# Six local-attention layers of a 2048-token kernel: the value path is folded into per-head weights and applied to the shifted input, and half of the softmax exponentials are taken straight from PSUM

## What is computed

```python
qkv = x @ Wqkv                     # 128 -> 3 * 1024; 16 heads of 64
q = l2norm(q) * qs ; k = l2norm(k) * ksc
q, k = rotary(q), rotary(k)
# windows of 32 queries, each with the 64 keys of its own and the window before
sim  = einsum(bq, bk2) * 8 ; sim = where(mask, -max, sim)
attn = softmax(sim)
out  = (attn @ bv2) @ Wo           # 1024 -> 128, added to x
x    = x + a * gelu(gate) @ W2 + b2     # after a layer norm and W1
```

## Time and profile before

| | |
|---|---|
| three runs | 2907.69, 2910.03 and 2917.73 us; median 2910.03 |
| span of the profiled execution | 2911.7 us |
| PE busy | 2789.5 us (96%) |
| DVE busy | 2336.3 us (80%) |
| ACT busy | 1746.4 us (60%) |
| POOL busy | 1680.3 us (58%) |

### The profile page before, as it was taken

How to read it: one execution, slowest core, us unless ns; L and a number is a source line. 1 busy time by engine, 2 the same in 40 slices (tenths; PEclk the granted TensorE clock), 3 DMA queues, 4 the chain that set the end, 5 groups by cost and what they waited for, 6 DMA issues and landing times.

```text
span 2911.7 us, 98296 instructions
## 1 busy us (share of the span) xinstructions
PE 2789.5 (96%) x40886; PEld 1832.5 (63%) x40886; DVE 2336.3 (80%) x3830; ACT 1746.4 (60%) x2618; POOL 1680.3 (58%) x1454
## 2 busy tenths in 40 slices
PE   8999999999999999899999999999999999999997
PEld 5556565655665655566656666666666666666665
DVE  6777755774677776998968999889998999898884
ACT  4455555555666665556666666666666666666663
POOL 1000002000466665676767888878887888788882
PEclk9999999999999999999999999999999999999999
DMA  3000000000011111243234434333443343333332
GB/s 97 1 1 1 1 1 3 1 1 10 21 45 46 45 46 31 77 129 79 73 103 106 99 86 114 84 93 88 114 95 91 92 118 91 88 89 83 89 85 66
DMA packets 183114, 188.24 MB, mean 65 GB/s; under 512 B 77517, under 2 KB 130515, under 8 KB 181139
## 3 DMA queue, kind: packets, MB, share of 16 engines
q1 hardware_dynamic: 182675, 181.94, 24.8%
HBM read 61.00 MB, written 6.03 MB: 23 GB/s over the span
## 4 chain that ended last, share of the span: by engine, by line
PE 73%; DVE 10%; issue 5%; POOL 5%; SPq 3%; ACT 3%; DMA 1%; DVEq 0%; POOLq 0%; ACTq 0%
PE ps L1348 13%; PE ps L587 13%; PE ps L1356 5%; PE ps L1400 5%; PE ps L1442 4%; PE ps L1363 4%; PE ps L622 4%; PE ps L600 4%; PE ps L1389 2%; PE ps L1456 2%; PE ps L1409 2%; PE ps L534 2%; PE ps L605 2%; PE ps L1457 2%; DVE nmx L695 2%
## 5 line engine op out<-in xcount | busy, mean ns | idle before, releaser
L1348 PE MATMUL ps<-wqkv,xcT 128*128 128x512 f32 x1152 | 553.2, 603 | 4.7 <-DVE area L1886 1.6
L587 PE MATMUL ps<-xnT,qp 128*128 128x512 f32 (+3 forms) x1280 | 527.1, 543 | 17.2 <-ACT prob L814 16.3
L2030 POOL TENSOR_TENSOR ra<-ra,rb 128x1024 f32<-128x1024 f32 x191 | 452.4, 2375 | 121.9 <-DVE rb L1854 121.0
L814 ACT ACTIVATE prob<-ps,ebias,shift 128x1024 f32<-128x1024 f32 (+7 forms) x384 | 360.3, 955 | 124.0 <-DVE ebias L704 60.4
L822 ACT ACTIVATE probT<-ps 128x512 f32<-128x512 f32 (+3 forms) x384 | 207.9, 541 | 353.6 <-PE ps L600 353.5
L587 PEld LDWEIGHTS ps<-xnT,qp 128*128 128x128 f32 x1280 | 231.7, 191 | 273.6 <-issue 228.5
L2049 POOL TENSOR_TENSOR ra<-ra,rn 128x1024 f32<-128x1024 f32 x192 | 362.3, 1908 | 8.9 <-DVE ra L1946 1.2
L695 DVE TENSOR_REDUCE nmx<-ps 128x1 f32<-128x1024 f32 (+7 forms) x256 | 245.8, 987 | 108.3 <-PE ps L587 93.3
L1348 PEld LDWEIGHTS ps<-wqkv,xcT 128*128 128x128 f32 x1152 | 196.7, 190 | 154.3 <-issue 143.5
L1630 ACT ACTIVATE sq<-ps 128x1024 f32<-128x1024 f32 x192 | 195.6, 1019 | 85.6 <-PE ps L1348 85.3
L1852 DVE TENSOR_TENSOR ra<-ps,tab 128x1024 f32<-128x1024 f32 x192 | 233.6, 1217 | 3.7 <-issue 3.1
(11 more groups left out here) (274 smaller groups left out, 5651.9 us busy)
## 6 DMA issues: line engine op xcount, KB each, us to landing
vw<-vs SPq DMA_DIRECT2D x576, 130.0 KB
vw<-vs SPq DMA_DIRECT2D x384, 65.0 KB
bc<-bc_scratch SPq DMA_DIRECT2D x128, 128.0 KB, 2.9
area<-bc_scratch SPq DMA_DIRECT2D x128, 128.0 KB, 4.3
wqkv<-lwqkv_dram SPq DMA_DIRECT2D x6, 1536.0 KB, 8.6
xc<-xs SPq DMA_DIRECT2D x96, 32.0 KB
wo<-lwo_dram SPq DMA_DIRECT2D x6, 512.0 KB, 9.6
xc<-xs SPq DMA_DIRECT2D x96, 31.8 KB
```

The costliest lines, as they stand in the source:

```text
L587: mm = E.matmul(ps[:, 2 * r + o // 512, 0:w], k.qp[:, group % 2, g % NTH * P:(g % NTH + 1) * P], k.xnT[:, k0 + o:k0 + o + w], start=True, ...
L814: A.activation(k.prob[:, r, 0:nk], ps[:, 2 * r:2 * r + 2, :].rearrange("p a b -> p (a b)")[:, 0:nk], ACT.Exp, bias=k.ebias[:, row % 2:row ...
L1348: mm = E.matmul(to[:, c, :], k.xcT[:, n % 4, :], k.wqkv[l % 2][:, at + 512 * c:at + 512 * (c + 1)], start=True, stop=True)
L2030: G.tensor_tensor(k.ra[:, n % 2, w, :], k.ra[:, n % 2, w, :], k.rb[:, w, :], ALU.add).then_inc(s("added_" + what), 1)
```

## The change

Values are no longer projected. Per layer and head the product of `Wv` and `Wo` (128x128) is formed once (`fold`); per tile the probabilities, normalised and transposed by DVE in blocks of 32x32, weigh the shifted input itself (`mix`: eight matmuls of 32 rows, 128 columns and 512 moving columns), and the 16 heads' results go through the 16 folded matrices in `side`. The first eight heads take their exponential from PSUM with the negated maximum as bias, one ACT instruction of 64 columns per head; for the other eight DVE subtracts as before. The rotary product is one DVE instruction of 2048 columns, POOL's sum two of 512. The sums of squares are one reduction. The bias b2 becomes a row of ones in the forward block's product (`FROWS`) and its POOL additions go. The copy of the recurrence's state goes from DVE to ACT (`state`). The orders of all queues and the PSUM pairs change with it, and the recurrence starts one step later (`FIRST_UNIT` 22 to 23).

```diff
@@ tables @@
-TAPS = {3: 3, 4: 3, 5: 3, 6: 2, 7: 3, 8: 3, 9: 2, 10: 2, 11: 3, 12: 3, 13: 2, 14: 1}
+TAPS = {4: 3, 5: 3, 6: 3, 7: 3, 8: 3, 9: 3, 10: 2, 11: 3, 12: 3, 13: 2, 14: 2}
-        a, b, c, d = (3, 1, 2, 0) if n % 2 else (0, 1, 2, 3)
...
+        a, b, c, d = (2, 3, 0, 1) if n % 2 else (0, 1, 2, 3)
+        table.update({("scores", n): a, ("q", n + 2): b, ("late", n): d, ("k", n + 2): c, ("extra", n): d, ("side", n): a, ("rows_q", n + 1): b, ("rows_k", n + 1): c,
+                      ("mix0", n): a, ("mix1", n): b})
+FOLDS = {0: (("late", 0, 0), ("extra", 0, 1))}
+FOLDS.update({NT * (l - 1) + 8 + half: (("late", l, half),) for l in range(1, L) for half in range(2)})
@@ PE @@
+    def scores(n):
+        to = pair(("scores", n), ("shifted_s", n + 1), ("exp_s", n + 1))
...
+    def fold(place, n, l, half):
...
+                mm = E.matmul(to[:, o, j * P:(j + 1) * P], k.wvT[at, 4 * half + j, :], k.wo[at, 4 * half + j, :], start=True, stop=True, skip_group_check=True)
+    def mix(n):
+        to = [pair((f"mix{i}", n), ("mixT", 2 * n + i + 1)) for i in range(2)]
+        E.wait_ge(s("prT"), n + 1)
...
+        for half in range(2):
+            for w in range(4):
+                at = slice(WIN * w, WIN * (w + 1))
+                of = k.xc[at, n % XRING, :] if half == 0 else k.xp[at, n % PRING, :]
+                mm = E.matmul(to[w // 2][:, w % 2, :], of, prT[at, :, 1 - half, :], start=half == 0, stop=half == 1, skip_group_check=True)
@@ PE, side @@
-            for c in range(8):
-                mm = E.matmul(to[:, 0, 0:P], k.oT[:, c * P:(c + 1) * P], k.wo[:, l % 2, c, :], ...)
+            for c in range(H):
+                mm = E.matmul(to[:, 0, 0:P], k.mixT[:, c, :, :].rearrange("p w q -> p (w q)"), k.wvo[:, l % 2, c, :], ...)
@@ PE, a step: scores, q, late, k, extra/forward, side, rows, mix @@
-            turn_probs(n)
-            project("v", n + 1, ("v_out", n + 2))
-            values(n, 0)
-            values(n, 1)
-            turn_out(n)
+            scores(n)
+            project_q(n + 2)
...
+            project_k(n + 2)
...
+        forward(n)
...
+            side(n)
...
+            mix(n)
@@ ACT, a step @@
+            mix_out(n - 1, 0)
+            mix_out(n - 1, 1)
             square("q", n + 2)
+                state(u)
             unit_decay(k, u)
...
             probs(n)
             square("k", n + 2)
-            values_out(n + 1)
...
-            out_turned(n)
             lengths(n + 2)
@@ ACT, probs @@
+        of = pair("scores", n)[:, 0, :]
+        A.wait_ge(s("top_s"), n + 1)
...
+        for j in range(8):
+            ins = A.activation(k.pr[:, j * DH:(j + 1) * DH], of[:, j * DH:(j + 1) * DH], ACT.Exp, bias=k.nmxl[:, n % 2, j:j + 1])
+        ins.then_inc(s("exp_s"), 1)
+        A.wait_ge(s("shifted_s"), n + 1)
+        A.activation(k.pr[:, 512:1024], k.pr[:, 512:1024], ACT.Exp).then_inc(s("exp"), 1)
@@ DVE @@
+    def normalise(n):
+        pr = k.pr[:].rearrange("p (h d) -> p h d", d=DH)
+        V.wait_ge(s("exp"), n + 1)
+        V.tensor_reduce(k.suml[:], pr, X_AXIS, ALU.add).then_inc(s("v"), k.v.up())
+        V.reciprocal(k.recl[:], k.suml[:]).then_inc(s("v"), k.v.up())
+        V.tensor_tensor(pr, pr, bcast(k.recl[:], 2, DH), ALU.mult).then_inc(s("v"), k.v.up())
...
+        V.transpose(k.prT[:], k.pr[:]).then_inc(s("prT"), 1)
@@ DVE, rotate @@
-        V.tensor_tensor(out_a, of, bcast(tab[:, 2 * w, :], 1, H), ALU.mult)
-        V.tensor_tensor(out_b[:, :, 0:32], ...)
-        V.tensor_tensor(out_b[:, :, 32:64], ...).then_inc(s("rotated_" + what), 1)
+        V.tensor_tensor(k.rot[:, n % 2, w, :, :].rearrange("p c (h d) -> p c h d", d=DH), bcast(heads(what, n), 1, 2),
+                        bcast(k.tab[:, n % FRAME, 2 * w:2 * w + 2, :], 2, H), ALU.mult).then_inc(s("rotated_" + what), 1)
@@ DVE, a step @@
+            scan(u)
             shift(n)
+            rotate("q", n + 2)
+            rotate("k", n + 2)
+            normalise(n)
             finish(n - 1)
...
+            gated(m, int(what[2]))
...
+            sum_squares(n + 2)
@@ POOL, add @@
-        G.tensor_tensor(k.ra[:, n % 2, w, :], k.ra[:, n % 2, w, :], k.rb[:, w, :], ALU.add).then_inc(s("added_" + what), 1)
+        G.tensor_tensor(a[:, :, 0:DH // 2], a[:, :, 0:DH // 2], b[:, :, DH // 2:DH], ALU.add)
+        G.tensor_tensor(a[:, :, DH // 2:DH], a[:, :, DH // 2:DH], b[:, :, 0:DH // 2], ALU.add).then_inc(s("added_" + what), 1)
@@ SP @@
-    def spread_values(n):
+    def keys_before(n):
+        S.wait_ge(s(f"xc{n % 2}"), 48 * (n // 2 + 1))
...
+            S.dma_start(k.xp[0:WIN, b, :], k.xc[P - WIN:P, (n - 1) % XRING, :]).then_inc(s(f"xp{n % PRING}"), 16)
+        S.dma_start(k.xp[WIN:P, b, :], k.xc[0:P - WIN, n % XRING, :]).then_inc(s(f"xp{n % PRING}"), 16)
```

More of the change, by code:

```diff
@@ L44 @@
 SCANS = 9060
-VALUE_HEADS = [2 * (2 * c + i) + o for i in range(2) for o in range(2) for c in range(4)]
-OUT_HEADS = [2 * (2 * c + i) + o for o in range(2) for i in range(2) for c in range(4)]
+XRING, PRING = 8, 4
 class Count:
@@ L1405, in turn_out @@
-    def turn_out(n):
-        to = pair(("turn_out", n), ("oT", n + 1))
-        E.wait_ge(s("on1"), n + 1)
-        for c in range(8):
-            mm = E.transpose(to[:, c // 4, c % 4 * P:(c % 4 + 1) * P], k.on[:, c * P:(c + 1) * P], k.ident[:])
-        mm.then_inc(s("out_turned"), 1)
+        for j in range(8):
+            for w in range(4):
+                for o in range(2):
+                    mm = E.matmul(to[WIN * w:WIN * (w + 1), o, j * DH:(j + 1) * DH], k.qT[o * DH:(o + 1) * DH, j, WIN * w:WIN * (w + 1)],
+                                  k.kT[o * DH:(o + 1) * DH, n % 2, j, WIN * w:WIN * w + DH], start=False, stop=True, skip_group_check=True)
@@ L1530, in project_in @@
     def project_in(place, n, m):
-        to = pair((place, n), ("in_out", 2 * m + 2))
+        to = pair((place, n), ("in_out", 2 * IN_ORDER.index(m) + 2))
         for q in range(2):
@@ L1669, in probs, with mix_out, state @@
     def probs(n):
-        for o in range(2):
-            here = k.pr[:, o * 512:(o + 1) * 512]
-            A.wait_ge(s("shifted_s"), 2 * n + o + 1)
-            A.activation(here, here, ACT.Exp).then_inc(s("exp"), 1)
-    def out_turned(n):
-        A.wait_ge(s("out_turned"), n + 1)
+        of = pair("scores", n)[:, 0, :]
+        A.wait_ge(s("top_s"), n + 1)
+        if n:
+            A.wait_ge(s("prT"), n)
+        for j in range(8):
+            ins = A.activation(k.pr[:, j * DH:(j + 1) * DH], of[:, j * DH:(j + 1) * DH], ACT.Exp, bias=k.nmxl[:, n % 2, j:j + 1])
+        ins.then_inc(s("exp_s"), 1)
+        A.wait_ge(s("shifted_s"), n + 1)
+        A.activation(k.pr[:, 512:1024], k.pr[:, 512:1024], ACT.Exp).then_inc(s("exp"), 1)
+    def mix_out(n, i):
+        A.wait_ge(s("mixed"), 2 * n + i + 1)
         if n:
             A.wait_ge(s("fin_mm"), n)
-        A.activation(k.oT[:], flat("turn_out", n), ACT.Copy).then_inc(s("oT"), 1)
+        A.activation(k.mixT[:, :, 2 * i:2 * i + 2, :].rearrange("p c w q -> p w c q"), pair(f"mix{i}", n).rearrange("p w (c q) -> p w c q", q=WIN), ACT.Copy).then_inc(s("mixT"), 1)
+    def state(u):
+        c, i, b = u // NS, u % NS, u % 2
+        A.wait_ge(s("scanned"), u + 1)
+        A.activation(k.last[:, i, :], k.hx[:, b, :, CH - 1], ACT.Copy).then_inc(s("state"), 1)
     def normal_turned(m):
@@ L1763, in transformer_act @@
             unit_decay(k, u)
-        if n + 3 < NTILE:
-            turned_input(n + 3)
-        if new_frame(n + 1) and n + 1 < NTILE:
-            halo_turned(n + 1)
+        if n in IN_LATE:
+            projected_in("late", n, IN_LATE[n])
+        if n == FACTOR_STEP:
+            factors(n)
+        if n in RATE_STEPS:
+            rates(n, RATE_STEPS[n])
+        for place, l, half in FOLDS.get(n, ()):
+            folded(place, n, l, half)
         if n < NTILE:
@@ L1994, in transformer_dve @@
             down(m - 1)
-        elif what and what != "turn_normal" and not gate_first:
-            gated(m, int(what[2]))
         if n == NTILE + 3:
@@ L2324 @@
     qs, ks = a["L1_ffn_q_scale"], a["L1_ffn_k_scale"]
-    turned = lambda v: np.concatenate([v[:, DH // 2:], v[:, :DH // 2]], 1)
-    by_heads = lambda v, axis, order: np.concatenate([np.take(v, range(DH * h, DH * h + DH), axis) for h in order], axis)
     b1 = np.zeros((L, P, 6), np.float32)
```

361 lines of the change are left out of this document (139 added, 222 removed).

## The result

The changed kernel takes 3150.34 us (four runs, 3146.01 to 3158.49) against 2912.2 us for the kernel before beside it: a ratio of 1.083 [1.080, 1.086], 238 us slower. The forecast was 3035 with a range to 3110. The direction was right, and the loss is nearly twice the one predicted.

The account below looks back on a forecast made before the run. PE bounds the kernel before; after the change a loop through PE, ACT and DVE would: 64 steps at 19.1 and 31 at 18.1 us, plus convolution and folds, 1813 against 1686, less 1.5 at the tail: 3035 us, range 2785 to 3110.

Parts of the forecast that it names:

- The loop closes: Links through PE, ACT and DVE run one after another each step: 19.1 us with a unit, 18.1 without; chance 0.49.
- the first rival: PE's or DVE's work, not the chain of waits, sets the step; with DVE at 16.5 us, 2795 us; chance 0.28.
- Both idle times: PE idle some 3 us ahead of each `mix`, DVE some 2 us ahead of the keys' rotary product.
- The gain of PE's shorter work: PE's work per step falls by 5.4 - 1.9 - 2.0 = 1.5 us.
- Line 1: Residual (`finish`), which frees the PSUM pair that `mix` takes, and its semaphore: 0.3 us.
- Line 2: `mix` on PE, eight 32-row matmuls of 512 columns: 2.0 us, ends 1.7 and 6.9.
- the fourth rival: `mix` row groups do not overlap, or idle PE gets its lower clock: over 3400 us; chance 0.05.
- Lines 3 and 4: On PE, mask and scores 2.1 us, then query projection to the end of its last result 1.98 us.
- line 7: Eight ACT exponentials of 64 columns: 2.0 us, at 0.25 us each, ends 0.21 and 0.30.
- Line 6: The recurrence's decays and state copy on ACT: 0.95 us together, only in steps that have a unit.
- Line 12: DVE's product of the probabilities, both inputs in SBUF, waits for POOL's sum: 1.05 us, ends 0 and 1.2.

Follow-up runs that it names:

- the edit of PE's order: Changed kernel with `side(n)` put ahead of `forward(n)` on PE in steps with n % 4 == 2, from step 6 on: 3101.87 us.
- the useless matmuls: Changed kernel with twelve extra bfloat16 matmuls of 512 columns on PE ahead of `mix`, results unused, in three steps of four: 3091.63 us.
- the experiment with the reduction: Changed kernel with DVE's product that divides the probabilities replaced by a sum of the same 1024 columns: 3029.1 us.
- the version of 2897 us: Changed kernel with keys' square ahead of the exponentials, one exponential of 1024 columns, and `side` early in steps with n % 4 == 2: 2897.15 us.

## Why the prediction was right, and where it failed

**The loop closes** (the forecast against the first rival): right in its mechanism. Both idle times that were to show it are there, and moving the keys' square alone brings 160 us. The gain of PE's shorter work was never collected.

The links, as mean distances over 92 steps of the trace (start to start; line 1 from the end of DVE's transpose to `mix`), beside the prediction's lines:

| lines of the prediction | predicted us | measured us |
|---|---|---|
| 1, from the transpose over the residual to `mix` | 0.3 | 0.98 |
| 2, `mix` | 2.0 | 2.59 |
| 3, mask and scores | 2.1 | 2.05 |
| 4, query projection, with its semaphore | 1.98 | 2.18 |
| 5 and 6, queries' square, decays, state | 1.85 | 1.77 |
| 7 and 8, the exponentials | 2.5 | 2.09 |
| 9, keys' square | 1.0 | 1.08 |
| 10, rotary product of the keys | 2.2 | 2.21 |
| 11, sum and reciprocal | 1.4 | 1.53 |
| 11 and 12, product with its wait | 2.25 | 2.34 |
| 11, transpose | 1.2 | 1.25 |
| 13, the semaphore not in a link | 0.3 | 0.09 |
| sum | 19.1 | 20.16 |

Two lines carry the miss.

**Line 1 failed.** It priced the residual at its own duration, 0.3 us, and did not ask when PE gets to what stands ahead of it. In three steps of four the distance is 0.28 us, as priced; in the steps with n % 4 == 2 it is 3.1 us in the mean, since `side` stands on PE behind a product that waits for POOL's layer norm, and the transposes and `mix` stand behind `side`. That is 23 x 2.8 = 64 us; the edit of PE's order gave back 48.

**Line 2 was mis-sized, and the fourth rival with it.** At the full clock `mix` takes 1.93 us, so the choice of 2.0 between 1.7 and 6.9 was right. But PE, idle about 3 us ahead of it, gets it at the lower clock in about half of the steps. The prediction had seen this idle time and named the lower clock, yet only as half of a rival of 0.05, in which lines 2 to 4 double in every step. It belonged into line 2 as a surcharge in part of the steps: 0.59 x 95 = 56 us; the useless matmuls gave back 59. Lines 3 and 4 stayed near their price in the mean, though mask and scores take 2.08 us in the median behind a slow `mix` and 1.70 behind a quick one.

These two make 120 us, against the 108 by which 1921 us exceeds the 1813 of the forecast. The others come to -18, the largest being these: the exponentials were 0.4 us cheaper a step (-39), since they follow each other 0.20 us apart, below the low end of line 7 (1.74 us for eight, the last 0.33 long), and the separate semaphores 0.2 (-20); the query projection with its semaphore was 0.2 dearer (+19), the other links of DVE together some 0.3 (+26). The few us left lie in the first and last steps.

So the plain step of the loop was priced too high. Outside n % 4 == 2 there are 20 steps with a unit, without a fold and with `mix` at the full clock; 13 of them take 18.1 to 18.3 us, not 19.1 (the others 18.5 to 22.7). The forecast was too low because of what comes on top in part of the steps. Line 6 is among what was right: steps 21, 39 and 93, plain ones without a unit, take 17.2 to 17.3 us, 0.9 less, and ACT goes from the square to the exponentials in 0.92 us in place of 1.81.

**Line 12 was right**, 1.06 against 1.05 us, by way of the earlier trace rows. So were the DVE transpose (1.25 for 1.2) and the 2048-column rotary product. That the mean came out so well is partly luck: most products wait 1.0 us, 12 hardly at all, and six wait 2.3 to 5.5, of which the prediction had nothing. The Trainium skill ("SBUF — State Buffer", Who interferes with whom) names the same contention for a VectorE instruction with two SBUF inputs, and the experiment with the reduction, which has one input, agrees: 1.22 us in all 96 cases.

**The range** ended at 3110 because its upper end let one line be 0.8 us longer. It should have held both a late queue and the clock. Idle time on PE is what the forecast itself had a loop make, so the lower clock belonged inside its range.

## What to carry to other kernels

When a change lets one engine's result feed back to itself within a step, list the links of that loop, and for each link what else must be there, which PSUM pair it holds and what is queued ahead of it: the same eight exponentials cost 6.5 us beside a full PE, 75 or 122 us in the loop. An order of two instructions on an engine that is busy 62% of the time was worth 160 us here, the clock that it gave back included. And price TensorE behind a wait at both of its clocks.

## What the runs showed of the hardware

- **A DVE product with two SBUF inputs can wait through many GpSimd instructions, not just one.** In the version of 2897 us, DVE's timeline and that of POOL:

```profile
2013.00 7.22 DVE L1822 TENSOR_TENSOR area<-area,recl 128x1024 f32<-128x1024 f32 x1
```

```profile
2012.97 1.27 POOL L2003 TENSOR_TENSOR rot<-rot 128x512 f32<-128x512 f32 x1
2014.21 1.27 POOL L2002 TENSOR_TENSOR rot<-rot 128x512 f32<-128x512 f32 x1
2015.44 1.26 POOL L2003 TENSOR_TENSOR rot<-rot 128x512 f32<-128x512 f32 x1
2016.66 1.25 POOL L466 TENSOR_TENSOR acc<-area 128x512 f32<-128x512 f32 x1
2017.88 1.26 POOL L490 TENSOR_TENSOR acc<-acc,area 128x512 f32<-128x512 f32 x1
2019.22 2.13 POOL L492 TENSOR_TENSOR area<-area,acc 128x512 f32<-128x512 f32 x1
```

  The product ends at 2020.22 and needs 1.22, so it began at 2019.0, after five instructions of POOL that follow without a gap; the next one is longer by 0.9 us in its turn. It is the worst of 96 (75 take under 1.5 us). The Trainium skill ("SBUF — State Buffer", Who interferes with whom) has whoever comes first hold the shared port for its whole instruction; the trace shows that the one that waits isn't always next. In the changed kernel a product at 2015.42 did come in after one. What decides it no run here shows.
- **The lower clock comes and goes within one step of 20 us**: 0.54 over a `mix` behind 3.2 us of idle time, 1.00 over the projections behind it.
- **Eight 32-row float32 matmuls of 512 columns, four side by side, take 1.93 us** at the full clock; by the 1.72 us of two full-size ones eight in a row would take 6.9, so the gain is 3.6 times. The Trainium skill ("TensorE: Matmul & The Clock Gate", Part 3) has 3.07 times for four row tiles of 32 with 512 columns; the measurement decides for this kernel.
- **A DVE transpose of 1024 float32 columns takes 1.25 us**, the time of a product of as many columns.
